# Keys and values of a linear attention: norm folded into weights, seven basis channels, values scaled from the accumulators

## The reference

```
qkv = xf @ qkv_w.T + qkv_b             # per pixel, 8 heads of 8 channels
k = w_k * (k - mean(k)) / (std(k) + eps) + b_k     # over the 8 channels of a head
v = w_v * (v - mean(v)) / (std(v) + eps) + b_v
kv = sum over the 16384 pixels of k^T v / N        # 8 x 8 per head and image
ret = q @ kv + x
out = gelu(ret @ o1.T + o1_b) @ o2.T + o2_b + x
```

## Time and profile before

| | |
|---|---|
| median of 3 runs | 2748.52 us (2747.4 to 2749.88) |
| the profiled execution | 2751.44 us, span 2749.6 us |
| PE busy | 2593.2 us, 94% |
| DVE, ACT, POOL busy | 1902.8, 1291.6, 140.2 us |
| granted TensorE clock, mean | 0.981 |

### The profile page before, as it was taken

One profiled execution on the slowest core, in us unless ns is written; L12 is line 12 of the kernel. 1 busy time (PEld: TensorE's weight loads), 2 busy tenths in 40 slices (PEclk: granted clock), 3 DMA queues, 4 the chain that ended last, 5 costly groups with the idle time before them and its releaser, 6 DMA issues.

```text
span 2749.6 us, 112371 instructions
## 1 busy us (share of the span) xinstructions
PE 2593.2 (94%) x42998; PEld 2468.8 (90%) x42998; DVE 1902.8 (69%) x6167; ACT 1291.6 (47%) x2564; POOL 140.2 (5%) x241
## 2 busy tenths in 40 slices
PE   2889999999999999996999999999999999959999
PEld 1279999999999999996999999999999999959973
DVE  7976666666666666677566666666666667779975
ACT  1656663222233333456666622223333334569979
POOL 1400000000000000000000000000000000003334
PEclk9999999999999999998999999999999999979999
DMA  6720001222300000025900012223000001230005
GB/s 256 179 71 0 0 0 35 61 61 61 96 0 0 0 5 0 0 77 149 329 0 0 0 50 61 61 61 81 0 0 0 0 0 31 61 92 0 0 8 237
DMA packets 158396, 146.02 MB, mean 53 GB/s; under 512 B 22738, under 2 KB 146068, under 8 KB 154260
## 3 DMA queue, kind: packets, MB, share of 16 engines
q1 hardware_dynamic: 146432, 142.65, 17.7%
q10 hardware_dynamic: 11924, 2.90, 0.5%
HBM read 61.61 MB, written 50.33 MB: 41 GB/s over the span
## 4 chain that ended last, share of the span: by engine, by line
PE 89%; DVE 3%; DMA 2%; issue 2%; ACT 2%; SPq 1%; ACTq 0%; POOL 0%; DVEq 0%; POOLq 0%
PE banks L687 80%; PE banks L738 4%; PE banks L749 2%; DVE state L902 1%; DMA state<-x_in 1%; PE banks L735 1%; DVE state L1010 1%; PE banks L660 1%; ACT hid L444 1%; DMA res<-resid 1%; SPq L254 1%; DMA resid<-state 0%; ACT state L450 0%; PE banks L629 0%; POOL state L383 0%
## 5 line engine op out<-in xcount | busy, mean ns | idle before, releaser
L687 PE MATMUL banks<-x_row,w_taps 128*64 128x124 f32 (+2 forms) x40640 | 2204.7, 270 | 12.8 <-DVE x_row L933 8.0
L687 PEld LDWEIGHTS banks<-x_row,w_taps 128*64 128x64 f32 x40640 | 2202.5, 135 | 14.9 <-DVE x_row L933 9.3
L933 DVE SCALAR_TENSOR_TENSOR x_row<-banks,sweep_nbias,biased_row 128x128 f32<-128x128 f32 x2032 | 713.2, 351 | 723.4 <-PE banks L687 708.8
L484 ACT ACTIVATE biased_row<-state,sweep_bias 128x256 f32 (+1 forms) x762 | 511.1, 671 | 1028.4 <-DVE state L936 591.7
L480 ACT ACTIVATE biased_row<-state,aff,gn_a 128x64 f32 (+1 forms) x1016 | 364.5, 429 | 184.8 <-DVE state L942 184.8
L936 DVE SCALAR_TENSOR_TENSOR state<-banks,sweep_nbias,biased_row 128x128 f32 (+1 forms) x1016 | 442.9, 436 | 0.2 <-issue 0.2
L942 DVE SCALAR_TENSOR_TENSOR state<-banks,sweep_nbias,biased_row 128x64 f32 (+1 forms) x1016 | 237.2, 275 | 0.2
L942 DVE SCALAR_TENSOR_TENSOR turn_ring<-banks,sweep_nbias,biased_row 128x64 f32<-128x64 f32 x1016 | 237.0, 275 | 0.0
L370 POOL TENSOR_TENSOR res<-res,ones 128x64 f32<-128x64 f32 x64 | 44.9, 702 | 2452.0 <-DVE res L1059 2452.0
L738 PE MATMUL banks<-kv_w,res 128*128 128x256 f32 x512 | 132.2, 381 | 0.0
L660 PE MATMUL banks<-hid,ffn_w 64*64 64x512 f32 x512 | 120.2, 611 | 11.6 <-DVE state L902 10.4
(11 more groups left out here) (116 smaller groups left out, 943.1 us busy)
## 6 DMA issues: line engine op xcount, KB each, us to landing
state<-turn_ring SPq DMA_DIRECT2D x512, 64.0 KB, 1.9
state<-x_in SPq DMA_DIRECT2D x16, 1024.0 KB, 21.0
resid<-state SPq DMA_DIRECT2D x64, 256.0 KB, 3.6
res<-resid SPq DMA_DIRECT2D x16, 1024.0 KB, 9.0
res<-resid SPq DMA_DIRECT2D x32, 512.0 KB, 5.4
resid<-state SPq DMA_DIRECT2D x16, 1024.0 KB, 11.7
out_y<-state SPq DMA_DIRECT2D x16, 1024.0 KB, 3.9
state<-resid SPq DMA_DIRECT2D x32, 256.0 KB, 9.1
```

Source lines behind the costliest of these rows:

```text
L484: nc.scalar.activation(as_cells(n, biased_row[:, k, :, :]), cells(n, slice(0, B), i, k, g), ACT.Identity, bias=sweep_bias[:, n:n + 1]).the ...
L687: last = nc.tensor.matmul(out_ps[blk, :, lo:hi], w_taps[:, n % 2, s, blk], x_row[c][src][:, :, s + lo:s + hi], start=at == 0, stop=at == T ...
L933: nc.vector.scalar_tensor_tensor(x_row[c][par][:, :, 2:2 + HALF], ps, nb, br, ALU.max, ALU.add).then_inc(row_ready[c], 1)
```

## The change

No staging: the group norm is folded into the weights, per image. DVE scales the basis weights by `gn_a` into `kvw_s`, and PE forms the bias from `gn_c` (`gnc_cols`), which ACT rounds and DVE splits in two into `bias_rows`. PE then reads `state` itself, each half of the rows alone, as 64-row products into a bank for each half.

The centring becomes a change of basis: seven orthonormal vectors (`helmert`, built on POOL) for each head, so 7 channels a group in place of 8, and 112 columns in place of 128. The sum of the squares over seven is the same variance.

ACT squares 896 elements and copies the keys alone; DVE scales v straight out of PSUM into `gram_kv`, so a pair of banks is free only when `kv_copied` and `v_scaled` both say so. There are three pairs (`KV_BANKS`), four slots in SBUF (`KV_SLOTS`), v is scaled two tiles late (`SCALE_LAG`) and the Gram four late (`GRAM_LAG`). Adding eps and multiplying the deviations go to POOL. The Gram becomes 16 products of 64 x 64 on the four quadrants of the array, into banks 6 and 7, which ACT and DVE add behind the loop. All loops over tiles are written out. `hid` moves into the ring, `gram_sb` out of it.

```diff
 # PE
+            pe.wait_ge(weights_folded, 1)
+            pe.wait_ge(basis_ready, 1)
+            for b in range(B):
+                at = bank[4][:, b * KVN:(b + 1) * KVN].rearrange("p (g e) -> p g e", e=HU)
+                nc.tensor.matmul(at, gnc_cols[:, b, :], helmert[0:C, 0, :, 0:HU], start=True, stop=False)
+                last = nc.tensor.matmul(at, ones[0:C, :].bitcast(F32), helmert[0:C, 2, :, 0:HU], start=False, stop=True)
+            last.then_inc(bias_products_done, 1)
...
+            def kv_products(n):
+                b, j = n % B, n // B
+                if n >= KV_BANKS:
+                    pe.wait_ge(kv_copied, n - KV_BANKS + 1)
+                    pe.wait_ge(v_scaled, n - KV_BANKS + 1)
+                for q in range(2):
+                    blk = slice(q * C, (q + 1) * C)
+                    nc.tensor.matmul(pair[n % KV_BANKS][:, q * BANK:(q + 1) * BANK].rearrange("p (t n) -> p t n", t=PARTS)[:, :, 0:KVN],
+                                     picks[blk, :], bias_rows[blk, b, :].unsqueeze(1).to_broadcast([C, PARTS, KVN]), start=True, stop=False)
+                for t in range(PARTS):
+                    top, w = t % 2 * P, j * (PARTS // 2) + t // 2
+                    for q in range(2):
+                        blk = slice(q * C, (q + 1) * C)
+                        col = q * BANK + t * P
+                        last = nc.tensor.matmul(pair[n % KV_BANKS][:, col:col + KVN], half_rows[blk, top:top + P, b, w],
+                                                kvw_s[blk, b, :], start=False, stop=t == PARTS - 1)
+                last.then_inc(kv_done, 1)
+            def gram(n):
+                b, slot_ = n % B, n % KV_SLOTS
+                pe.wait_ge(v_scaled, n + 1)
+                pe.wait_ge(v_tails_ready, n + 1)
+                pe.wait_ge(kv_copied, n + 1)
+                for t in range(PARTS):
+                    for q in range(2):
+                        for r in range(2):
+                            rows_, u = slice(r * C, (r + 1) * C), q * PARTS + t
+                            last = nc.tensor.matmul(bank[6 + r][q * C:(q + 1) * C, b * C:(b + 1) * C],
...
+            pe.wait_ge(bias_ready, 1)
+            for n in range(KV_TILES):
+                if n == KV_BANKS - 1:
+                    operands()      # products of uv with wq, o1_t and q_col
...
+                kv_products(n)
+                if n >= GRAM_LAG:
+                    gram(n - GRAM_LAG)
 # ACT
+            for n in range(KV_TILES):
+                kv_square(n)        # waits kv_done n+1, group_sums_ready n-1
+                if n:
+                    kv_root(n - 1)  # waits group_sums_ready n
+                kv_copy(n)          # keys alone; waits gram_done n-3
 # DVE
+            def kv_sum(n):
+                dve.wait_ge(kv_squared, n + 1)
...
+            def kv_scale(n):
+                slot_ = n % KV_SLOTS
+                dve.wait_ge(scale_product_ready, n + 1)
+                nc.vector.reciprocal(rkv[:, slot_, :], dprod[:, slot_, :]).then_inc(inverse_ready, 1)
+                dve.wait_ge(inverse_ready, n + 1)
+                if n >= KV_SLOTS:
+                    dve.wait_ge(gram_done, n - KV_SLOTS + 1)
...
+                nc.vector.tensor_tensor(gram_kv[:, slot_, :, 1, :, 0:HU], v, by, ALU.mult).then_inc(v_scaled, 1)
+            for n in range(KV_TILES):
+                kv_sum(n)
+                if n >= SCALE_LAG:
+                    kv_scale(n - SCALE_LAG)
 # POOL
+            for n in range(KV_TILES):
+                tails(n)            # waits deviation_ready n+1; eps, product of deviations
+                if n:
+                    scaled_tail(n - 1)  # waits inverse_ready n
```

## The result

The changed kernel takes 2908.14 us (2905.78 to 2912.58) against 2749.2 us of the kernel before, a ratio of 1.058 (95% interval 1.0562 to 1.0598): 159 us more, where 147 more and 2895 us were forecast. The profiled execution's span is 2910.6 us, 161.0 over that of before.

The account below looks back on a forecast made before the run. It took a ring of waits, one tile a trip, as the bound: fourth tile at 2468.0, 60 trips x 5.54 = 332.4, tail 9.4, last Gram at 2809.8 against 2663.7, plus 0.8: +147 us, 2895 us; range 2828 to 2940.

Parts of the forecast that it names:

- The ring: Key/value loop: a tile's products wait for the previous tile's sum and an older tile's scaling; one tile a trip, 5.54 us.
- The parts outside PE: Key/value loop: square, sum, reciprocal and scaling with their hand-overs, 3.34 us a trip, already over the 3.08 of before.
- The busy times: Key/value loop: every engine's work a tile falls below 3.08 us, seeming a gain, but the order of waits matters more.
- The clock: Key/value loop: PE's pauses keep it at 1.2 GHz for nearly all of it; trip 5.54 us against 4.55 at full clock.
- PE's part: Key/value loop: bias, paired products and their end in each trip, 1.21 us at full clock, 2.2 at the lower.
- Rival 1: Key/value loop: clock stays at 2.4 GHz, 4.55 us a trip, 2835 us; chance 20%.
- Rival 2: Key/value loop: row halves don't overlap; trip 5.51 us at full clock, 7.5 at the lower, 3012 us; lower-clock chance 8%.
- two routes: Key/value loop: lower clock, trip 5.54 us and 2895 us, or weight loads at full clock, trip 5.5 and about 2892.
- 60 trips: Key/value loop after the fourth tile starts: 60 x 5.54 = 332.4 us.
- Filling: Start of the key/value loop: the fourth tile starts about 9 us after the first bias product could.
- The free parts: Key/value loop: Gram, ACT's copy and root, and POOL's tails run beside the trip, PE being free 3.34 us of each.
- The change of mode: Key/value loop: two tiling-mode changes a tile drain PE but fall into its free time; no price added.

Follow-up runs that it names:

- Experiment 1: Changed kernel with DVE scaling tile n-2 ahead of the sum of tile n instead of behind it: 2743.9 us, 0.9986 of the kernel before.
- experiment 2: Changed kernel with ACT copying keys and values, DVE scaling v in SBUF, and a bank pair free once copied: 2724.4 us, 0.9911 of the kernel before.
- experiment 3: Changed kernel with seven more unread products behind every Gram to fill PE's pause: 2903.24 us, 1.0562 of the kernel before.
- experiment 4: Changed kernel with tile products streaming only the 56 key columns of 112, weight loads untouched, output wrong: 2907.62 us in one execution.
- experiment 9: experiment 2 with each stationary operand read from 128 consecutive elements a partition, output wrong: 2692.01 us, 0.9797 of the kernel before.
- experiment 5: experiment 2 with each 64 x 128 product cut into two of 64 x 64 on quadrants: 2700.07 us, 0.9828 of the kernel before.

## Why the prediction came out as it did

**The ring: right, and shown.** Products, square, sum, and the reciprocal and scaling of tile n-3, one tile a trip. The parts outside PE were put at 3.34 us and are 0.95 + 1.00 + 0.58 + 0.77 = 3.30 in the chain at 2600 to 2603. Experiment 1 opens the ring by order, experiment 2 by buffer; each takes away over 160 us.

**The busy times: right that they don't decide.** In experiment 2, where no ring closes, the pace is the busiest engine's, 2.67.

**The clock: the reason failed, the number survived.** The step "PE's part is 2 x 0.96 + 0.28 = 2.2, the trip 5.54" took the products to run in pairs, bound by columns: 0.75 us at full clock, 1.5 at the lower one. Rival 1 put the clock at 59 us by it. The products take 1.72 at the lower level and 1.73 in a trip begun at the upper; only the bias halves differ (0.74 and 0.48). Filling the pauses gave 5 us in all (experiment 3). The clock wasn't low for nearly all of it either but averaged 0.59: it rose behind the unbroken 3.4 us from 2603.2 and stood at 1.00 through the pause and the next start.

**What stood in its place:** the stationary side. The 16 products took 1.72 us at the lower level, 1.65 at the upper (experiment 2) and 1.60 with half the columns (experiment 4). Rival 2 comes near in one figure only: its halves take turns but are still bound by their columns, which gives PE's part 2.17 at full clock (2.23 measured) and 4.1 at the lower one (2.48 measured), so its 3012 us fell with its reason.

The figure in the prediction that fits is the estimate from the Trainium skill (TensorE: Matmul & The Clock Gate, LDWEIGHTS), that a load's time goes by its columns and not its rows: 1.7 us for 16 loads and 2892 us. The two rows set beside it there are both of 64 rows and say nothing about rows. The changed kernel's trace does: at the lower clock a load of 128 columns lasts 306 ns with 64 rows (L820) and 313 with 128 (L668).

So two routes led to nearly one figure, and the wrong one was taken. That my 2.2 for PE's part lies near the measured 2.48 and 2.23 is luck. Nor is the count of columns the whole: packed, the same 16 loads of 128 columns take 0.8 us less (experiment 9). The Trainium skill's rule (same section) has no term for the stride; the 0.104 a load that fits it so well in the strided case is not shown to be its mechanism. By an estimate from the Trainium skill's rule (same section, 0.107 us for 128 columns), the 0.05 a record of the packed case would be two loads side by side, which no run here shows.

**The sum, term by term.** 60 trips: 342.5 us (2471.53 to 2814.07, 5.709 each) against 332.4. From the end of `gn_c` to the first product: 6.9 against 5.9; the bias products and the subtractions took longer, and `keep_warm` products stood ahead in PE's program, so that the first product started 0.7 us after the bias was ready. Filling: 11.1 against 9, since the first tiles' products went out at 2.1 to 2.5 each and the third sum waited 0.62 for its square. The group norm ended 1.4 earlier, 1.8 forecast. Tail from the last tile's start: 8.8 against 9.4. Behind the last Gram 87.7 to the end against 85.9: +1.8, forecast +0.8; the products of `gram_sb` (L824) ran at 0.50 and took 2.09, where those of before (L776) ran at 1.00 and took 1.16. Together 161 of span, 147 forecast; most of the difference, 10 us, is the trip's 0.17 us.

**The free parts.** Gram, keys' copy, root and tails stayed beside the trip: PE still paused 2.28 us in each, and the chain never passes through any of them.

**The change of mode.** I took none into the sum and said that it would fall into PE's free time. In the ring nothing on the chain waited for the Gram, so it could cost nothing there. Where PE is the bound it shows: 32 Gram records take 0.46 behind quadrant products (experiment 5) and 0.62 behind products of 64 x 128 (experiment 2). In experiment 5 the Gram's loads start 0.12 ahead of its first product, in experiment 2 together with it. The 0.16 us fits the Trainium skill's drain at a change of tiling mode (TensorEngine Tiling (Array Packing), Key Properties). No run separates it from other causes.

## What to carry to other kernels

Before counting busy time, write down for each buffer who frees it and what stands ahead of the freeing instruction on its engine: a lag of two tiles with three buffers gave no overlap at all, and swapping two calls gave it back. An operation saved (a copy of 448 elements on an engine with slack) may be what let a scarce buffer go early. And a read in place saves a staging copy but may read the stationary operand with a stride; compare with a packed one before believing the count of columns.

## What the runs showed of the hardware that was not expected

- A stationary operand read at one element every 512 bytes is slow: 16 products of 64 x 128 take 1.65 us strided, about 0.8 less packed; 8 products of 128 x 128 with 224 columns 2.03 strided, 1.71 packed. How the time goes with other strides wasn't tried.
- Quadrant products stand the stride better at full clock (1.38 us for 32) than row halves (1.65 for 16), but not at the lower clock (1.78 and 1.72). Why is open: loads of 64 columns, or four places to overlap in.
- 32 Gram records of 64 x 64 x 64 end in 0.46 us, 0.014 us each, behind quadrant products, and in 0.62 behind products of 64 x 128.
